# Moving a pair's first probability transposes behind its last V tile, and putting its two weighted sums side by side

## The reference

```python
q = (layernorm(x) @ Wq.T + bq); k = (ctx @ Wk.T + bk); v = (ctx @ Wv.T + bv)   # 16 heads of 32
scores = einsum('bhqd,bhkd->bhqk', q, k) / sqrt(32) + mask                     # keys: 257
attn = softmax(scores, axis=-1)
x = x + einsum('bhqk,bhkd->bhqd', attn, v).reshape(B, S, 512) @ Wo.T + bo
```

## Time and profile before

| | us |
|---|---|
| median of 3 runs | 824.67 (821.84 to 825.98) |
| the profiled execution: its time | 823.83 |
| the profiled execution: its span, first to last instruction | 822.0 |
| TensorE busy, share of the span | 93% |
| VectorE, ScalarE, GpSimd busy | 47%, 41%, 24% |
| mean granted TensorE clock | 0.982 of 2.4 GHz |

### The profile page before, as it was taken

One profiled execution on the slowest core, in us unless ns is written; L12 is line 12 of the kernel. 1 busy time (PEld: TensorE's weight loads), 2 busy tenths in 40 slices (PEclk: granted clock), 3 DMA queues, 4 the chain that ended last, 5 costly groups with the idle time before them and its releaser, 6 DMA issues. The chain is left out here.

```text
span 822.0 us, 20581 instructions
## 1 busy us (share of the span) xinstructions
PE 763.2 (93%) x8258; PEld 587.7 (71%) x8258; DVE 387.3 (47%) x938; ACT 336.2 (41%) x688; POOL 195.4 (24%) x247
## 2 busy tenths in 40 slices
PE   2999999999999999999999998679999989999994
PEld 1777787777777777877777676557888767677673
DVE  6614333424342433334243426466666577433546
ACT  2533434444453544354444535323545454721220
POOL 2005000000000000000000101456677672493002
PEclk9999999999999999999999999889999999999998
DMA  8111110110111011101101113130000003100011
GB/s 328 52 53 53 53 50 4 53 51 5 46 51 51 0 51 51 51 0 51 51 10 41 51 51 102 53 93 2 1 0 0 0 13 132 39 0 1 1 52 51
DMA packets 9320, 36.95 MB, mean 45 GB/s; under 512 B 2617, under 2 KB 2873, under 8 KB 6210
## 3 DMA queue, kind: packets, MB, share of 16 engines
q1 hardware_dynamic: 9282, 36.42, 12.7%
HBM read 34.32 MB, written 2.10 MB: 44 GB/s over the span
## 5 line engine op out<-in xcount | busy, mean ns | idle before, releaser
L94 PE MATMUL pj<-W_hi 128*128 128x512 f32 x512 | 210.2, 411 | 0.0
L96 PE MATMUL pj<-W_lo,W_hi 128*128 128x512 f32 x512 | 200.6, 392 | 0.0
L95 PE MATMUL pj<-W_hi,W_lo 128*128 128x512 f32 x512 | 199.4, 390 | 0.0
L94 PEld LDWEIGHTS pj<-W_hi 128*128 128x128 f32 x512 | 96.1, 188 | 31.4 <-issue 13.2
L96 PEld LDWEIGHTS pj<-W_lo,W_hi 128*128 128x128 f32 x512 | 96.0, 188 | 21.9
L230 POOL COPY q_b<-Q_T 128x128 f32 (+1 forms) x32 | 9.3, 291 | 420.8 <-PE tp L350 372.7
L95 PEld LDWEIGHTS pj<-W_hi,W_lo 128*128 128x128 f32 x512 | 96.4, 188 | 17.8
L461 ACT ACTIVATE K<-pj,bk 128x512 f32<-128x512 f32 x64 | 44.2, 690 | 136.9 <-PE pj L96 136.9
L628 DVE CUSTOM_DVE_ANT_0 m_flat<-sc,mask 128x257 f32<-128x257 f32 x64 | 25.3, 424 | 127.2 <-PE tp L350 102.9
L476 ACT ACTIVATE p_flat<-m_flat,nmax 128x257 f32<-128x257 f32 x128 | 63.8, 501 | 24.3 <-DVE nmax L628 24.2
L468 ACT ACTIVATE V<-pj 128x512 f32<-128x512 f32 x64 | 38.3, 598 | 74.7 <-PE pj L96 72.7
(11 more groups left out here) (268 smaller groups left out, 1369.0 us busy)
## 6 DMA issues: line engine op xcount, KB each, us to landing
raw<-ctx_dram SPq DMA_DIRECT2D x15, 1024.0 KB, 4.8
raw<-w_dram SPq DMA_DIRECT2D x6, 768.0 KB, 4.8
raw<-w_dram SPq DMA_DIRECT2D x4, 1024.0 KB, 4.8
out_dram<-raw SPq DMA_DIRECT2D x8, 256.0 KB, 2.1
x_nat<-x_dram SPq DMA_DIRECT2D x2, 512.0 KB, 4.7
raw<-wq_dram SPq DMA_DIRECT2D x1, 1024.0 KB, 7.2
x_nat<-x_dram SPq DMA_DIRECT2D x1, 1024.0 KB, 9.2
raw<-wk_dram SPq DMA_DIRECT2D x1, 1024.0 KB, 10.6
```

Source lines behind the costliest of these rows:

```text
L94: eng.matmul(out, a_hi, b_hi, start=first, stop=False)
L95: eng.matmul(out, a_lo, b_hi, start=False, stop=False)
L96: return eng.matmul(out, a_hi, b_lo, start=False, stop=last)
```

## The change

In TensorE's list `transposes(n, 0)` moves from ahead of the last V tile to behind it, and `weighted_sum(n-1, 1)` from behind K2 to right behind `weighted_sum(n-1, 0)`. To let the second sum start before the first has been taken out, the second writes into columns 128 to 255 of bank `pb`, and waits until `otail` of its batch has been read out of that bank (`ot_made`). The next tail matmul into `pb` waits for both sums of the pair before to have been taken out (`o_out`). `dtail` gets one buffer for each batch of the pair. On ScalarE `v_evac(n, 3)` and `pt_evac(n, 0)` change places, on VectorE `pt_evac(n, 0)` and `normalise(n, 1)`. The work itself, in instructions and sizes, stays the same.

```diff
-        dtail = sb("dtail", [P, CT, S])
+        dtail = sb("dtail", [P, 2, CT, S])
+        context_of = (po[:, 0:P], pb[:, P:2 * P])
@@ transposes
                 eng.wait_ge(dt_made, b + 1)
                 need(eng, ot_made, b)
-                eng.matmul(pb[:, 0:P], same_head[:, :], dtail[:, :, :].rearrange("p g s -> p (g s)"),
+                need(eng, o_out, 2 * n)
+                eng.matmul(pb[:, 0:P], same_head[:, :], dtail[:, j, :, :].rearrange("p g s -> p (g s)"),
@@ weighted_sum
-                need(eng, o_out, b)
+                need(eng, o_out, b - 1)
+                if j == 1:
+                    eng.wait_ge(ot_made, b + 1)
-                            mm = eng.matmul(po[h * HD:(h + 1) * HD, g * S:(g + 1) * S], V[:, 2 * j + k, cols],
+                            mm = eng.matmul(context_of[j][h * HD:(h + 1) * HD, g * S:(g + 1) * S], V[:, 2 * j + k, cols],
@@ TensorE, pair
                     weighted_sum(n - 1, 0)
+                    weighted_sum(n - 1, 1)
                 else:
                     tails()
                 k_tile(n, p, 2)
-                if not first:
-                    weighted_sum(n - 1, 1)
-                else:
+                if first:
                     tail_transposes()
@@
                 v_tile(n, p, 2)
+                v_tile(n, p, 3)
                 transposes(n, 0)
-                v_tile(n, p, 3)
@@ ScalarE, pair
+                v_evac(n, 3)
                 pt_evac(n, 0)
-                v_evac(n, 3)
@@ VectorE, normalise
-                need(eng, pb_done, b)
+                need(eng, pb_done, b - 1)
@@ VectorE, o_evac
-                eng.tensor_tensor(O_T[:, :, bass.ds(b * S, S)], po[:, 0:P].rearrange("p (g s) -> p g s", g=CT),
+                eng.tensor_tensor(O_T[:, :, bass.ds(b * S, S)], context_of[j].rearrange("p (g s) -> p g s", g=CT),
@@ VectorE, pair
                 normalise(n, 0)
+                normalise(n, 1)
                 pt_evac(n, 0)
-                normalise(n, 1)
```

More of the change, by code:

```diff
@@ L640, in normalise @@
                 eng.wait_ge(probs_made, 4 * (b + 1))
-                need(eng, pb_done, b)
-                eng.tensor_tensor(dtail[:, :, :], same_q[:, :].unsqueeze(1).broadcast_to([P, CT, S]),
+                need(eng, pb_done, b - 1)
+                eng.tensor_tensor(dtail[:, j, :, :], same_q[:, :].unsqueeze(1).broadcast_to([P, CT, S]),
                                   probs[:, j, :, SM:SK].broadcast_to([P, CT, S]), ALU.mult).then_inc(dt_made, 1)
```

## The result

The changed kernel takes 811.35 us (median of 4 runs, 810.86 to 812.90) beside 823.25 us before (median of 4, 821.73 to 825.98). The ratio is 0.9849, 95% interval 0.9829 to 0.9868: 12 us faster. Predicted was 814.0 in a range of 810.5 to 819.5. The profiled execution took 810.86 us with a span of 809.1, where before had 823.83 and 822.0.

The account below looks back on a forecast made before the run. TensorE was taken as the bound, busy 139.63 of 141.00 us in five pairs. Stops 8.6 plus sums 2.2 less 0.5 at pair 15's end made 10.3 us off: 814 us stated, range 810.5 to 819.5.

Parts of the forecast that it names:

- The stops: TensorE's stops ahead of transposes(n, 0), pairs 0 to 14, vanish once V3 runs first: 8.6 us gained.
- What is late next: VectorE's copy of batch 0 and transposes(n, 1): slacks of 1.6 and 1.8 us, so no new stop.
- The sums: Two weighted sums side by side save one visit to 128 x 32 tiles in each of 15 pairs: 2.2 us.
- rival 3: The side-by-side sums lose to their waits: -1.5 us in place of +2.2, result 818; chance 0.06.
- The end of pair 15: VectorE's weight_split(1) delays the copy of batch 1, so the second sum and the end come 0.5 us later.
- Rival 1: TensorE's loop branch, now behind transposes, stalls in the open: 6 branches x 1.0 us, result 820; chance 0.08.
- Rival 2: Clock falls at pair 15's end, slowing the next block's first 12 matmuls: 2.4 us, result 816.5; chance 0.05.

Follow-up runs that it names:

- the sums apart: Changed kernel with the second weighted sum moved back behind K2, the transposes still behind V3: 815.37 us, ratio 0.9896.
- the six extra operations: Changed kernel with six extra 128 x 512 VectorE operations, their output unread, between normalise(n, 1) and pt_evac(n, 0): 825.34 us, one run.
- the sums before the scores: Changed kernel with both weighted sums moved from behind K1 to between V0 and scores(n, 0): 814.88 us, ratio 0.9883.
- VectorE's split on GpSimd: Changed kernel with the low half of the next block's second weight made by GpSimd instead of VectorE in pair 15: 811.21 us, ratio 0.9853.
- the kernel with the waits first: Changed kernel with both sums between V0 and scores, VectorE's split on GpSimd, and the scores' six waits passed ahead of the sums: 810.12 us, ratio 0.9828.
- the block-by-block kernel: Kernel before, order untouched, each of the first four probability blocks transposed once its own scaling is done: 817.05 us, ratio 0.9908.
- second profile: Changed kernel itself run once more, on one chip with three other kernels: 813.17 us, ratio 0.9861.

## Why the prediction was right, and where it was off

The mechanism held at each step; the sum was 10.3 us, the profile shows 12.88 in the stretch it was made for. The two terms that were too small err the same way, so 811.35 lies inside the range but just below the 812 to 816.5 to which the prediction gave 0.72: no rival made the kernel faster than that, the gain was underpriced. The lower end of the range came near it by a slip: from the median 824.67 the working gives 824.67 - 10.8 - 3 = 810.9, not 810.5.

- **The stops, 8.6 us.** Nothing is left of them, in any pair. With the sums apart the stretch is 9.18 us shorter, and with the 0.46 us of the end put back the term is 9.6. The missing 1.0 us: transposes behind a stop run 0.90 to 0.94 us, not 0.87, which I had seen and priced at nothing (0.5 us in 15 pairs), pair 1 has a stop of 0.27 us, of which the records show 0.11 idle, too little for the list of waits to count; the remaining 0.2 is rounding and the spacing of the tiles behind a stop.
- **What is late next: nothing.** Forecast was a slack of 1.6 us for VectorE ahead of its copy (measured 1.64) and 1.8 behind it (2.0 by the six extra operations).
- **The sums, 2.2 us.** Measured 3.75. This is the term that was mis-sized, and twice in the same direction. The visit costs 0.25 us, not 0.18: I counted only the first and last gap, and the matmuls behind a return to the big tiles stand 0.23 to 0.24 apart instead of 0.227. And I took off a pass of waits between the sums by a row in which TensorE stood still; behind work of its own it passes the five waits, two instructions in its queue, almost free (0.72 us from sum to sum beside 0.69 from a sum to a tile). That rival 3's cost exists all the same is shown by the sums before the scores: 0.42 us a pair, where six instructions stand in the queue. The Trainium skill, "TensorEngine Tiling (Array Packing)", Key Properties, says that a change of tiling mode drains TensorE. For a change from and to 128 x 128 the traces agree, at 0.25 us for both ways; between 128 x 32 and 32 x 32 they show no price beyond the ordinary.
- **The end of pair 15, -0.5 us.** Measured -0.46, and for the named reason: VectorE's split on GpSimd takes the second sum's wait from 1.21 to 0.16 us.
- **Rival 1, the turn of the loop.** Behind transposes(5, 0) of 1.01 us, K0 starts at 215.27 with no stop, and takes 2.83 us as in the pairs without a branch. The trace's records of transfers say more: none of kind "instruction" runs on any queue between 157 and 453 us, and TensorE's six turns (the first at 157.7, one in 54.8 us) all lie in there, so the loop ran from what had been loaded. The Trainium skill, "Runtime: NRT & Kernel Launch", Instruction fetch mechanics, expects a stall at a taken branch whose target is not in the fetched window; by the records that case did not arise, and no trace here shows a stall at the turn. A stop that looks like it came at another place, once, in the kernel with the waits first.
- **Rival 2, the clock.** It exists, and it struck in 6 of the 14 profiles: the granted clock falls to 0.50 within 0.9 us of the next block's start. The changed kernel's second profile is one of them, its first is not, and the block-by-block kernel, whose end of pair 15 is in the old order, is another. With transposes(15, 0) behind V3 it is 4 of 10, ahead of it 2 of 4. So the change alone doesn't decide it. The chance of 0.05 was low against that. The price of 2.4 us holds as an upper end: in the second profile eight of the first spacings are wider, 1.6 us in sum.

## What to carry to other kernels

Where one engine is the bound and never idle long, look for its small stops start to start, since durations that overlap hide a third of each; a move by one tile pays when the late engine has room for what then comes next. First ask whether the wait is too coarse: four waits for four parts in place of one gave 7.5 of the 9.2 us of the move and changed no order. Passing a wait is free under long instructions and not always under short ones, so count the instructions that the waits become and put those of a group of short matmuls ahead of the work before it.

## What the runs showed of the hardware

**Passing waits costs time of its own.** Behind 128 matmuls of 32 columns six waits long fulfilled cost TensorE 0.15 us against constants and 0.42 against registers; under a tile of 512-column matmuls they cost none. What counts is the number of instructions in its queue, 0.10 to 0.11 us from start to start: two between the sums, behind the 64 matmuls of the first, cost 0.03, three 0.15, six 0.42. An estimate from these rows is 0.10 us for each, less some 0.18 that the matmuls ahead cover; the waits-first kernel moved all six at once and no run moves a single one. A stopped TensorE starts its transposes 0.24 us behind the data, a running one was there 0.10 us behind.

**The clock goes with the spread of the runs.** The second block took 314.0 to 318.7 us in profiles that share its code. Its mean granted clock was 0.953 in the four profiles of 314.0 to 314.6, and 0.938 or less in the five of 316.4 to 318.7. One fits badly, with 317.0 at 0.948, so the clock is not shown to be all of it. The changed kernel's two profiles differ there. Windows at the start of the next block (length, busy time and count of TensorE's matmuls and loads, VectorE, ScalarE and GpSimd, granted clock, DMA share, GB/s), first profile:

```profile
495.00:498.00 3.00, 2.91 (x13) 2.40 (x14) 0.00 (x0) 2.44 (x2) 1.90 (x3) 1.00 1.01 362
```

Second profile:

```profile
495.00:498.00 3.00, 3.00 (x9) 2.33 (x9) 0.00 (x0) 2.23 (x2) 1.86 (x2) 0.57 1.10 381
```

TensorE had stood still ahead of both for the same time, 1.21 and 0.80 us in the first, 1.17 and 0.81 in the second. Both start the block at 2.4 GHz. The first is still there at 498 us; in the second the clock falls to 1.2 GHz 0.57 us into the block and is back 3.4 us later. TensorE's timeline of the second shows it in the spacing, 0.23 us and then 0.40, and 0.43 from there on:

```profile
495.15 0.40 PE L95 MATMUL pw<-W_hi,o_first_lo 128*128 128x512 f32 x1
495.38 0.60 PE L96 MATMUL pw<-W_lo,o_first_hi 128*128 128x512 f32 x1
495.78 0.63 PE L94 MATMUL pw<-W_hi,o_first_hi 128*128 128x512 f32 x1
```

A gain of 1 us in the first stretch is lost in this spread, and only a comparison stretch by stretch shows it.
